# Set-up of a four-layer graph network: own rows' blocks masked out of loaded rows, own sums 100 columns wide, and zero rows up to 128

## What is computed

```python
x = _layernorm(x + L0(x, adj))     # adj @ (x @ weight) + bias
x = _layernorm(x + L1(x, adj))     # five node groups of the first 25 nodes: two normalised convolutions each
x = _layernorm(x + L2(x, adj))     # attention: adj * exp(e_i + f_j), rows divided by their sums
x = _layernorm(x + L3(x, adj))     # 17-tap convolution, distance-weighted messages, gated update
# in L3:
s = x @ w_se.T + b_se              # three columns
dist = sq[:, :, None] + sq[:, None, :] - 2.0 * jnp.einsum('bnd,bmd->bnm', s, s)
A = jnp.exp(-dist) * mask
msg = jax.nn.relu(x @ w_msg.T + b_msg)
```

## Time and profile before

| | us |
|---|---|
| median of 3 runs | 648.75 (646.16 to 649.4) |
| the profiled execution | 646.53 |
| its span, first to last instruction | 644.7 |
| TensorE busy | 605.6 (94%) |
| TensorE weight loads | 494.5 (77%) |
| VectorE busy | 491.4 (76%) |
| ScalarE busy | 314.0 (49%) |
| GpSimd busy | 111.8 (17%) |
| mean granted TensorE clock | 0.961 |

### The profile page before, as it was taken

The page is one execution under the profiler, slowest core; times in us unless marked ns, Lnnn a source line. Parts: engine busy times, 40 slices in busy tenths (PEclk is TensorE's granted clock), DMA queues, the critical chain, the costliest instruction groups (busy, mean ns, idle before and its releaser), DMA issues.

```text
span 644.7 us, 11585 instructions
## 1 busy us (share of the span) xinstructions
PE 605.6 (94%) x3553; PEld 494.5 (77%) x3553; DVE 491.4 (76%) x1833; ACT 314.0 (49%) x635; POOL 111.8 (17%) x118
## 2 busy tenths in 40 slices
PE   3799798999999999999999999999999999999893
PEld 2689686878797879797878787878787887879672
DVE  4547653878888888878888889797979797978753
ACT  2201363464646465556464645555464646464331
POOL 2410101121121212030212120212121212112100
PEclk9757898999999999999999999999999999999998
DMA  7880002200303030303030303030201102000000
GB/s 193 244 262 2 1 1 89 91 1 1 100 2 98 0 98 0 98 0 98 0 98 0 98 0 98 0 96 2 70 28 40 58 22 78 6 13 1 18 17 16
DMA packets 33522, 34.50 MB, mean 54 GB/s; under 512 B 1882, under 2 KB 22753, under 8 KB 33368
## 3 DMA queue, kind: packets, MB, share of 16 engines
q1 hardware_dynamic: 33154, 34.03, 17.1%
q10 hardware_dynamic: 342, 0.15, 0.1%
HBM read 29.79 MB, written 4.39 MB: 53 GB/s over the span
## 4 chain that ended last, share of the span: by engine, by line
PE 44%; issue 22%; DVE 11%; POOL 3%; ACT 3%; DVEq 0%; POOLq 0%; ACTq 0%
PE bank L247 6%; PE bank L249 5%; PE bank L248 5%; PE pair L247 4%; PE pair L249 4%; PE pair L248 4%; PE bank L1582 4%; POOL rs L1085 3%; PE pair L1518 3%; DVE x L1236 2%; DVE st L1219 2%; PE bank L1453 2%; PE bank L1485 2%; PE bank L1523 1%; DVE mv L1225 1%
## 5 line engine op out<-in xcount | busy, mean ns | idle before, releaser
L1085 POOL TENSOR_TENSOR rs<-ve,neg_half 128x4 f32<-128x4 f32 (+1 forms) x61 | 58.1, 952 | 332.4 <-DVE ve L1231 299.6
L247 PE MATMUL bank<-cd_hi,w_hi 128*128 128x256 f32 x272 | 81.3, 299 | 0.0
L249 PE MATMUL bank<-cd_hi,w_lo 128*128 128x256 f32 x272 | 76.8, 282 | 0.0
L248 PE MATMUL bank<-cd_lo,w_hi 128*128 128x256 f32 x272 | 76.7, 282 | 0.0
L247 PEld LDWEIGHTS bank<-cd_hi,w_hi 128*128 128x128 f32 x272 | 51.6, 190 | 11.8 <-issue 11.7
L1582 PE MATMUL bank<-P,msg 128*128 128x512 f32 x128 | 57.6, 593 | 0.2 <-issue 0.2
L247 PE MATMUL pair<-aT_hi,x_hi 128*128 128x512 f32 x128 | 52.3, 409 | 0.0
L248 PE MATMUL pair<-aT_lo,x_hi 128*128 128x512 f32 x128 | 51.6, 403 | 0.0
L248 PEld LDWEIGHTS bank<-cd_lo,w_hi 128*128 128x128 f32 x272 | 51.5, 189 | 0.0
L249 PE MATMUL pair<-aT_hi,x_lo 128*128 128x512 f32 x128 | 51.5, 402 | 0.0
L249 PEld LDWEIGHTS bank<-cd_hi,w_lo 128*128 128x128 f32 x272 | 51.3, 189 | 0.0
(11 more groups left out here) (326 smaller groups left out, 1543.0 us busy)
## 6 DMA issues: line engine op xcount, KB each, us to landing
adj_nat<-in_adj_dram SPq DMA_DIRECT2D x16, 1024.0 KB, 5.8
x_nat<-in_x_dram SPq DMA_DIRECT2D x16, 256.0 KB, 3.0
out_dram<-y_out SPq DMA_DIRECT2D x16, 256.0 KB, 2.4
xt<-in_x_dram SPq DMA_DIRECT2D x3, 1280.0 KB, 10.3
hw<-in_L_gnn_W_dram SPq DMA_DIRECT2D x2, 640.0 KB, 14.2
xt<-in_L_gnn_conv_w_dram SPq DMA_DIRECT2D x1, 1088.0 KB, 6.9
aT<-in_adj_dram SPq DMA_DIRECT2D x5, 150.0 KB
nat_ih<-in_L_gnn_w_ih_dram SPq DMA_DIRECT2D x1, 384.0 KB, 5.2
```

What stands on the lines that cost most here:

```text
L247: nc.tensor.matmul(o, lh, rh, start=start, stop=False)
L248: nc.tensor.matmul(o, lh, rl, start=False, stop=False)
L249: return nc.tensor.matmul(o, ll, rh, start=False, stop=stop)
L1085: g.tensor_tensor(rs[i][:, 0:n], ve[i][:, 0:n], neg_half[:, 0:n], ALU.pow).then_inc(po_rs[i], 1)
```

## The change

**Blocks of the own rows.** The six small DMAs and the clearing of `A0` are gone. GpSimd makes a mask `BD` of the five diagonal blocks, which VectorE multiplies into `GM` once. `AB` holds the first 25 columns of each own row, taken from `adj_nat` and `adjP` with the identity added, and `mask_blocks` spreads these 25 columns five times while it applies `GM`. So the blocks of the tiles 1 to 3 now wait for `adjP`. `mask_blocks` is called at three places instead of in one run of 15.

**Own sums.** Each own-sum matmul takes 100 moving columns, those of four graphs, of which 25 are the wanted ones. `copy_sums` picks these out with two ScalarE instructions instead of one.

**Zero rows.** `LR`, `msg_bias` and `ones_r` get 128 partitions. `LR` is cleared once by GpSimd after the barrier, and the distance matmul contracts over 128 rows instead of 13, the bias matmul over 128 instead of 64.

**Order.** Almost every list of the set-up is written in another order. On SP the loads of `fw`, `hb2` and `ab_col` come ahead of `hw2`. The first aggregation comes before the transposes of `adjP`. The second aggregation comes after all own sums instead of between those of the last tile. The weight transposes 2 and 3 and the transposes of graph 1's adjacency, chunks 2 and 3, move into the loop of the groups, each later `LATE` block moves on by one group, and chunk 1 moves behind `hidden(0)`. The scaling of the convolution's weights moves on VectorE from before the own outputs to just before the loop, and their pair sums `nat_sum` from VectorE to GpSimd.

```diff
-        msg_bias = sb("msg_bias", [64, 2, DM], f32r)
-        ones_r = sb("ones_r", [64, 128], f32r)
+        msg_bias = sb("msg_bias", [128, 2, DM], f32r)
+        ones_r = sb("ones_r", [128, 128], f32r)
...
-        A0 = flat1[:, 0:NT * R].rearrange("p (t n) -> p t n", t=NT)
-        CM = flat1[:, 512:512 + NG * R].rearrange("p (g n) -> p g n", g=NG)
-        GM = flat1[:, 1152:1152 + NG * R].rearrange("p (g n) -> p g n", g=NG)
+        CM = flat1[:, 0:NG * R].rearrange("p (g n) -> p g n", g=NG)
+        GM = flat1[:, 640:640 + NG * R].rearrange("p (g n) -> p g n", g=NG)
+        BD = flat1[:, 1280:1280 + R]
+        EY = flat1[:, 1408:1408 + NODES]
+        AB = flat1[:, 1440:1440 + NT * NODES].rearrange("p (t n) -> p t n", t=NT)
...
-        LR = sb("LR", [GR, 2, N], f32r)
+        LR = sb("LR", [128, 2, N], f32r)
...
-        W_BANK = [bank[i] for i in (4, 1, 4, 6, 5, 0, 1, 6, 5, 0)]
+        W_BANK = [bank[i] for i in (4, 4, 1, 6, 5, 0, 1, 6, 5, 0)]
         TT_BANK = [bank[4], bank[7], bank[0]]
-        LATE = [[4], [5], [6, 7], [8], []]
+        LATE = [[], [2, 3], [4, 5], [6, 7], [8]]
...
-                sp.wait_ge(q_zero, 1)
-                sp.dma_start(A0[0:NODES, 0, 0:NODES], a["adj"][0, 0:NODES, 0:NODES]).then_inc(q_blk, 16)
-                for j in range(PJ):
-                    sp.dma_start(A0[NODES * j:NODES * (j + 1), 1:NT, NODES * j:NODES * (j + 1)],
-                                 rows[j, 0:NODES, :, 0:NODES]).then_inc(q_blk, 16)
...
-                sp.dma_start(hw1[:, :, :], a["L1_gnn_W1"].rearrange("g i h -> i g h")).then_inc(q_h, 16)
-                sp.dma_start(hw2[:, :, :, :], a["L1_gnn_W2"].rearrange("g (h p) o -> p g h o", h=2)).then_inc(q_h, 16)
+                sp.dma_start(hw1[:, :, :], a["L1_gnn_W1"].rearrange("g i h -> i g h")).then_inc(q_h1, 16)
...
+                sp.dma_start(hw2[:, :, :, :], a["L1_gnn_W2"].rearrange("g (h p) o -> p g h o", h=2)).then_inc(q_h2, 16)
+                sp.wait_ge(q_zero, 1)
...
-                g.memset(A0, 0.0).then_inc(q_zero, 1)
+                g.memset(BD, 1.0)
+                g.memset(nat_se[:, :], 0.0).then_inc(q_zero, 1)
...
+                BD3 = BD[0:R].rearrange("p (j n) -> p j n", j=PJ)
+                g.affine_select(out=BD3, in_=BD3, compare_op=ALU.is_ge, fill=0.0, base=0,
+                                pattern=[[-NODES, PJ], [0, NODES]], channel_multiplier=1).then_inc(q_bd, 1)
+                pool.wait_ge(q_bd, 1)
+                g.affine_select(out=BD3, in_=BD3, compare_op=ALU.is_ge, fill=0.0, base=NODES - 1,
+                                pattern=[[NODES, PJ], [0, NODES]], channel_multiplier=-1).then_inc(q_bd, 1)
...
+                g.tensor_tensor(nat_sum, nat_c2[:, :, 0:TAPS - 1:2], nat_c2[:, :, 1:TAPS:2], ALU.add).then_inc(q_sum, 1)
...
-                    s.activation(TTs[:, t, :], TT_BANK[t][:, 0:R], ACT.Identity).then_inc(q_TTs, 1)
+                    s.activation(TTs[:, t, 0:R - NODES].rearrange("p (j n) -> p j n", n=NODES),
+                                 TT_BANK[t][:, 0:(PJ - 1) * R].rearrange("p (j n) -> p j n", n=R)[:, :, 0:NODES], ACT.Identity)
+                    s.activation(TTs[:, t, R - NODES:R], TT_BANK[t][:, (PJ - 1) * R - NODES:(PJ - 1) * R], ACT.Identity
+                                 ).then_inc(q_TTs, 1)
...
+                act.wait_ge(pe_agg1, 1)
+                s.activation(agg_sb[:, :], AG_BANK[:, :], ACT.Identity).then_inc(ac_agg1, 1)
                 copy_rows(0)
                 copy_rows(1)
-                act.wait_ge(pe_agg1, 1)
-                s.activation(agg_sb[:, :], AG_BANK[:, :], ACT.Identity).then_inc(ac_agg1, 1)
...
+                copy_sums(1)
+                round_weights(-1)
+                copy_sums(2)
...
-                copy_sums(1)
-                round_weights(-1)
...
+                round_weights(0)
+                act.wait_ge(pe_agg2, 1)
+                s.activation(agg_sb[:, :], AG_BANK[:, :], ACT.Identity).then_inc(ac_agg2, 1)
...
+                def mask_blocks(t):
+                    for gi in range(NG):
+                        last = v.tensor_tensor_reduce(A5[0:R, t, gi, :].rearrange("p (j n) -> p j n", j=PJ),
+                                                      bc(AB[0:R, t, :], PJ),
+                                                      GM[0:R, gi, :].rearrange("p (j n) -> p j n", j=PJ), 1.0, 0.0,
+                                                      ALU.mult, ALU.add, deg[0:R, 3, NG * t + gi:NG * t + gi + 1])
+                    return last
...
+                v.tensor_tensor(GM[0:R, :, :], GM[0:R, :, :], bc(BD[0:R], NG), ALU.mult).then_inc(q_gm, 1)
...
-                v.tensor_tensor(A0[0:R], A0[0:R], bc(ident[0:R, 0:R], NT), ALU.add).then_inc(q_A1, 1)
...
+                v.tensor_tensor(AB[0:NODES, 0, :], adj_nat[0][0:NODES, 0, 0:NODES], ident[0:NODES, 0:NODES], ALU.add
+                                ).then_inc(q_A1, 1)
...
+                v.tensor_tensor(AB[0:R, 1:NT, :], adjP[0:R, :, 0:NODES], bc(EY[0:R], PT), ALU.add).then_inc(q_A1, 1)
+                hold(dve, q_A1, 3)
+                mask_blocks(1)
...
-                            last = t_.matmul(TT_BANK[t][:, NODES * j:NODES * (j + 1)], xt[t][:, j, mc, :],
-                                             aPT[t % 2][:, mc, NODES * j:NODES * (j + 1)], start=(mc == 0), stop=(mc == NC - 1))
+                            lo = 0 if j < PJ - 1 else NODES
+                            last = t_.matmul(TT_BANK[t][:, 100 * j:100 * (j + 1)], xt[t][:, j, mc, :],
+                                             aPT[t % 2][:, mc, lo:lo + 100], start=(mc == 0), stop=(mc == NC - 1))
...
-                pe.wait_ge(q_adjP, 16 * PJ)
-                transpose_rows(0)
-                transpose_rows(1)
+                pe.wait_ge(q_gm, 2)
...
+                pe.wait_ge(q_adjP, 16 * PJ)
+                transpose_rows(0)
+                transpose_rows(1)
...
+            g.memset(f(LR[:, :, :]), 0.0).then_inc(po_LR0, 1)
...
+                    if not prev:
+                        act.wait_ge(po_LR0, 1)
...
-                    t_.matmul(AT_BANK[mc % 2][:, :], LR[0:KD, 0, ch(mc)], LR[0:KD, 1, :], start=True, stop=True
+                    t_.matmul(AT_BANK[mc % 2][:, :], LR[:, 0, ch(mc)], LR[:, 1, :], start=True, stop=True
```

More of the change, by code:

```diff
@@ L522, in _ @@
                         relu_hidden(gi + 1)
+                    for mc in LATE_AT[gi]:
+                        split_second(mc)
                     for k in LATE[gi]:
@@ L634, in _ @@
                                 spread(deg[0:NODES, 3, 0:NG], NODES), ALU.mult).then_inc(q_nT, 1)
-                dve.wait_ge(q_colsb, 1)
-                dve.nop(nofuse=True)
-                for j in range(2):
-                    last = v.tensor_scalar(abc[:, j, :], ones[:, :], cols[:, A1 + j:A1 + j + 1], None, ALU.mult)
-                last.then_inc(q_abc, 1)
+                mask_blocks(2)
                 hold(dve, po_rs[0], 1)
@@ L646, in _ @@
                 last.then_inc(dv_x1r, 1)
+                mask_blocks(3).then_inc(q_A5, 1)
+                degrees(R, NG, NT * NG, 2)
+                dve.wait_ge(q_colsb, 1)
+                dve.nop(nofuse=True)
                 v.tensor_scalar(bn_bias[:, :], cols[:, V1:V2 + 1:V2 - V1], EPS, None, ALU.add).then_inc(q_bnv, 1)
-                inverse_degrees(R, NG, NT * NG, 2)
-                for t in range(1, NT):
-                    v.tensor_tensor(A5[0:R, t], A5[0:R, t], spread(deg[0:R, 3, NG * t:NG * (t + 1)], R), ALU.mult).then_inc(q_B, 1)
+                for j in range(2):
+                    last = v.tensor_scalar(abc[:, j, :], ones[:, :], cols[:, A1 + j:A1 + j + 1], None, ALU.mult)
+                last.then_inc(q_abc, 1)
                 dve.wait_ge(q_cst2, 16 * 3)
@@ L696, in _ @@
                 last.then_inc(q_own, 1)
+                scale_columns(1)
                 dve.wait_ge(q_own, 5)
@@ L761, in _ @@
                 v.tensor_scalar(veP[0:R, :], mvP[0:R, :, 1], EPS, None, ALU.add).then_inc(q_nP, 1)
+                scale_columns(2)
+                scale_columns(3)
+                v.tensor_tensor(nadjT[0:R, 1:NT, 4, :], bank[3][0:R, 0:PT * R].rearrange("p (a b) -> p a b", a=PT),
+                                spread(deg[0:R, 3, NG + 4:NT * NG:NG], R), ALU.mult).then_inc(q_nT, 1)
+                rest_of_weights(0)
+                hold(dve, q_rsP, 1)
+                for t in range(PT):
+                    last = v.tensor_scalar(x1P[0:R, t, :], x1P[0:R, t, :], mvP[0:R, t, 0:1], rsP[0:R, t:t + 1], ALU.subtract,
+                                           ALU.mult)
+                last.then_inc(q_nP, 1)
+                for c in range(NC):
+                    last = dot(0, c)
+                last.then_inc(dv_e, 1)
                 hold(dve, pe_out2, 1)
@@ L774, in _ @@
                 last.then_inc(dv_y3, 1)
+                rest_of_weights(1)
+                rest_of_second(0)
                 hold(dve, dv_y3, 1)
                 first_statistics(2, lambda c: y3[:, c, :])
-                rest_of_weights(0)
```

(36 more changed lines are left out.)

216 lines of the change are left out of this document (99 added, 117 removed).

## The result

The changed kernel takes 615.15 us at the median (613.61 to 616.21, four runs); the kernel before, run beside it, 648.12 us (646.16 to 649.4). The ratio is 0.949, with a 95% interval from 0.946 to 0.953. Faster was right; 628.7 us was not, and 615 lies outside the range of 620 to 639. The gain is 33 us where 20 were forecast.

The account below looks back on a forecast made before the run. TensorE bounds the turns at full clock; the set-up loses time to half clock and waits. Set-up gain 20.7 less 0.7 for hops, turns 0: 648.75 - 20.0 = 628.7 us, range 620 to 639.

Parts of the forecast that it names:

- Turns, zero rows: Distance and bias matmuls over 128 rows in the turns: value 0, bounds -3.2 to +3.5 us.
- Steps 1 and 2: Set-up: first aggregation and layer output done by 19.5 us, gain 7.8; graph 0's hidden layer by 29.0, gain 13.7.
- Step 3: Set-up, VectorE sets the pace: own sums end at 45.4 us, second aggregation runs from 48.1 to 51.0.
- Steps 4 and 5: Set-up: `y3` done at 58.0 us, gain 15.9; first second-layer of the own rows at 60.9, gain 24.2.
- Step 6, the loop of groups: End of set-up: loop takes 20.4 us with added transposes, copies and remainders, ending at 81.3, gain 20.7.
- The rival that it costs only its transposes: Loop of groups: ScalarE and VectorE keep up, 18.0 instead of 20.4 us, 626.3 us in all; chance 0.10.
- the 0.7 us for hops: Set-up: 0.7 us taken off the gain for hops between engines that the sum leaves out.
- The clock held at 100 columns: Rival on set-up's own sums: clock does not hold at 100 columns, gain 10, 638.7 us; chance 0.12.
- Transfers bound only the start: Rival on set-up loads: transfers become the bound, landing 2 to 4 us late, gain 15, 633.7 us; chance 0.12.
- The distance matmul with 128 rows did not cost more: Rival "slower" in the turns: 128 rows cost more, at twice the time 656.9 us; chance 0.03.

## Why the prediction was wrong, point by point

**Turns, zero rows: value 0, bounds -3.2 to +3.5 us. This step failed, by 9.4 us.** It compared the lengths of records (442 with 392 ns) and took their difference for the price of the rows. A record's length holds what overlaps with its neighbours; on an engine that is full, a matmul costs the distance between starts. The note under the profile before says as much of records, and the prediction used the distance for the aggregation's products, but not here. The trace of before had it, round the first pair of a turn, matmul and loads:

```profile
185.84 0.28 PE L249 MATMUL bank<-cd_hi,w_lo 128*128 128x256 f32 x1
186.05 0.73 PE L1453 MATMUL bank<-LR 13*128 13x512 f32 x2
186.71 0.39 PE L247 MATMUL bank<-cd_hi,w_hi 128*128 128x256 f32 x1
186.93 0.28 PE L248 MATMUL bank<-cd_lo,w_hi 128*128 128x256 f32 x1
```

```profile
186.04 0.29 PEld L1453 LDWEIGHTS bank<-LR 13*128 13x128 f32 x2
186.70 0.19 PEld L247 LDWEIGHTS bank<-cd_hi,w_hi 128*128 128x128 f32 x1 [0.37 <-issue]
```

From 185.84 to 186.93 are 1.09 us; after needs 0.12 + 0.23 + 0.23 + 0.12 = 0.70 for the same. The bias matmul was waved through with "goes the same way"; it is half of the turns' gain, 0.36 of 0.67 us. The sentence that more rows gain nothing since the clock is full mixed up clock and work.

**Steps 1 and 2.** First aggregation ended at 15.3 (forecast 16.4). The layer output was computed until 22.25, not 19.5: `adjP` landed at 18.65 instead of 17.4, and the transposes and the output fell into 3.41 us of half clock. The hidden layer ended at 30.70 instead of 29.0. The order worked as forecast. The landing was mis-sized by 1.25 us: the loads of `adjP` were issued 2.3 us earlier than before (from 1.85 instead of 4.13), and landed 0.7 earlier, not 2.0. So it was with `xt` of tile 0, issued at 3.8 instead of 8.3 and landed after 17.9 us instead of 14.2, at 21.8 and not at 20.5. And the half clock made transposes and output 3.6 us long instead of 2.1.

**Step 3.** Own sums ended at 46.6 (45.4), with 0.114 us a record (0.118); the second aggregation ran from 48.95 to 51.95 (48.1 to 51.0). The late start of step 2 was partly absorbed.

**Steps 4 and 5.** `y3` ended at 57.76 (58.0), the first second-layer started at 60.09 (60.9).

**Step 6, the loop of groups: mis-sized.** It took 18.3 us (60.09 to 78.37), not 20.4. The rival that it costs only its transposes had 18.0, and it is the one that came true. In 60.09 to 76.94 TensorE is busy 16.69 of 16.85 us and VectorE 15.43: the two ran side by side, and the waits that I put between engines were not there. With the 0.7 us for hops, which were not needed, and the earlier start, this makes the set-up's 23.7 instead of 20: 2.1 + 0.8 + 0.7 = 3.6. With the 9.4 us of the turns this is 13.0 of the 13.6 us by which 628.7 was off.

**Rivals.** The clock held at 100 columns. Transfers bound only the start: `adjP` came late, and where the clock held there, `xt` was next, by 1 us and not by the 5 of that rival. The distance matmul with 128 rows did not cost more, it cost less: of that mechanism I had only priced the side on which it loses. The rival's 626.3 us less 9.4 of the turns is 616.9, 1.8 us above what was measured.

## What to carry to other kernels

On a full engine, price a matmul by the steps between starts, its own and its two neighbours', and not by the length of its record; and look whether its weight load lies beside the matmul before. A matmul with 13 to 64 rows among matmuls with 128 paid 0.2 us at each change here, and with zero rows up to 65 or 128 it paid nothing. How much of such a price arrives depends on the waits behind it: of the bias matmul's all arrived in the time, of the distance matmuls' two fifths. Where TensorE is busy with small matmuls of few moving columns, widening them at the same record time kept its clock; and a step that costs nothing by itself still decides at which clock the next one runs.
